# Recurrence step of a fused two-layer kernel: the power's exponent split in two, and the carrier's matmuls doubled into two PSUM banks

## The reference

```python
h_carrier = h.mean(axis=1)                      # over the 256 channels
T = cos((phase(xr_t) - phase(h_carrier)) / 2) ** 2
alpha = exp(dt_t * A_neg)
expo = 1 + (1 - alpha) * 0.5 * (1 - T)
mag, ph = c_mag(h), c_phase(h)                  # c_mag: sqrt(re^2 + im^2 + 1e-8)
cmag = minimum(exp(expo * log(mag + 1e-8)), 10)
h = from_polar(cmag, ph) + B_t * (dt_t * x_t)
h = from_polar(tanh(c_mag(h)), c_phase(h))
y_t = einsum('bnc,bdnc->bd', C_t, h)
```

## Time and profile before

| | |
|---|---|
| median of 3 runs | 12826.88 us (12825.58 to 12827.23) |
| the profiled execution | 12837.53 us |
| its span, first to last instruction | 12835.7 us |
| busy: DVE, ACT, PE, PEld | 76%, 64%, 45%, 33% |
| mean granted PE clock | 0.613 of full speed |

### The profile page before, as it was taken

One profiled execution on the slowest core, in us unless ns is written; L12 is line 12 of the kernel. 1 busy time (PEld: TensorE's weight loads), 2 busy tenths in 40 slices (PEclk: granted clock), 3 DMA queues, 4 the chain that ended last, 5 costly groups with the idle time before them and its releaser, 6 DMA issues. The chain is left out here.

```text
span 12835.7 us, 220415 instructions
## 1 busy us (share of the span) xinstructions
PE 5755.6 (45%) x52526; PEld 4270.2 (33%) x52542; DVE 9759.4 (76%) x56587; ACT 8162.1 (64%) x42451; POOL 94.5 (1%) x164
## 2 busy tenths in 40 slices
PE   5222222222222222222222222222237978888998
PEld 5222222222222222222222222222234546653335
DVE  5777777777777777777777777777774948868875
ACT  6666666666666666666666666666663732264665
POOL 0000000000000000000000000000000100000000
PEclk8555555555555555555555555555558979998999
DMA  1000100001000000001000010000100000011100
GB/s 56 14 14 14 21 14 14 14 14 21 14 14 14 18 17 15 14 14 20 16 14 14 14 21 14 14 14 14 21 10 12 1 23 6 1 37 48 31 24 21
DMA packets 339459, 227.53 MB, mean 18 GB/s; under 512 B 27662, under 2 KB 324183, under 8 KB 337884
## 3 DMA queue, kind: packets, MB, share of 16 engines
q1 hardware_dynamic: 338140, 213.30, 7.8%
HBM read 187.41 MB, written 25.43 MB: 17 GB/s over the span
## 5 line engine op out<-in xcount | busy, mean ns | idle before, releaser
L534 PE MATMUL scan_p_car<-scan_hs,scan_mean_mat 32*32 32x2 f32 x16392 | 579.6, 198 | 6583.9 <-DVE scan_hb L661 6571.2
L534 PEld LDWEIGHTS scan_p_car<-scan_hs,scan_mean_mat 32*32 32x32 f32 x16392 | 403.7, 136 | 6762.8 <-DVE scan_hb L661 6749.9
L579 ACT ACTIVATE scan_act_ps<-scan_act_ps 128x64 f32<-128x64 f32 (+1 forms) x8193 | 1635.1, 200 | 65.5
L579 ACT ACTIVATE scan_act_ps<-scan_state_ps 128x64 f32<-128x64 f32 x2048 | 426.0, 208 | 1879.4 <-DVE scan_state_ps L658 1879.4
L561 PE MATMUL scan_p_y<-scan_c_masked,scan_hb 128*64 128x4 f32 x16384 | 1234.2, 253 | 0.0
L539 PE MATMUL scan_p_car<-scan_eps_row,ones 1*128 1x3 f32 x4102 | 1197.9, 360 | 39.1 <-DMA scan_a_log<-L_attn_a_A_log 38.9
L661 DVE SCALAR_TENSOR_TENSOR scan_uw<-scan_w,scan_rsq 128x64 f32<-128x64 f32 x2048 | 461.4, 225 | 853.4 <-ACT scan_rsq L579 853.4
L561 PEld LDWEIGHTS scan_p_y<-scan_c_masked,scan_hb 128*64 128x64 f32 x16384 | 1055.4, 216 | 34.2
L539 PEld LDWEIGHTS scan_p_car<-scan_eps_row,ones 1*128 1x128 f32 x4102 | 1020.4, 308 | 72.0 <-DMA scan_a_log<-L_attn_a_A_log 39.3
L579 ACT ACTIVATE scan_power_ps<-scan_state_ps,scan_s 128x64 f32<-128x64 f32 x2049 | 591.1, 288 | 673.3 <-DVE scan_s L684 673.3
L658 DVE TENSOR_TENSOR scan_c<-scan_V,scan_power_ps 128x64 f32<-128x64 f32 x4096 | 723.7, 218 | 366.8 <-ACT scan_power_ps L579 304.7
(11 more groups left out here) (450 smaller groups left out, 17412.8 us busy)
## 6 DMA issues: line engine op xcount, KB each, us to landing
scan_step_in<-scan_scratch SPq DMA_DIRECT2D x520, 256.0 KB, 6.2
qk_scratch<-qkv_parts SPq DMA_DIRECT2D x32, 384.0 KB, 2.5
attn_qT<-qk_scratch SPq DMA_DIRECT2D x192, 64.0 KB, 2.2
attn_kT<-qk_scratch SPq DMA_DIRECT2D x192, 64.0 KB, 2.2
scan_scratch<-prep_dts SPq DMA_DIRECT2D x32, 256.0 KB, 2.1
x<-L_attn_a_x SPq DMA_DIRECT2D x1, 4096.0 KB
out<-x SPq DMA_DIRECT2D x1, 4096.0 KB
filter_in_taps<-c_kT SPq DMA_DIRECT2D x1, 2048.0 KB
```

The lines of the kernel that those rows point to most:

```text
L534: last = nc.tensor.matmul(p_car[slot][rows, 0:2], mean_mat[rows, :], hs[rows, :], start=False, stop=True)
L579: nc.scalar.activation(dst, src, func, **kw).then_inc(counts[par]["act"], 1)
```

## The change

The exponential's argument is split: `exp(-(alpha - 5) * lm / 4)` becomes an ACT instruction of its own (`pw`), and the rest, `exp((alpha - 1) * lm * dot * rs)` (the quarter is in the table behind `dot`), takes `rs` itself as pointer scale. `s` goes; DVE gets `t = (alpha - 5) * lm` and `X = dl * dot` (pointer scalar `dot`, written to PSUM). `F` and the wide `V` go; in their place are `Vr0`, `Vr1` (state times `ru`) and `V0`, `V1` (times `pw`), and `hp` is gone since `Vr0` adds the epsilon itself. `lm` moves ahead of `nsq` on ACT, and `mag` is written to PSUM. The carrier's four matmuls are made twice, into a bank for ACT and one for DVE, so `dot` waits for PE's `carrier2` in place of ACT's `nsq`. Both banks are seeded each step by two `epsilon` calls, behind `nsq` and `dot` and ahead of `y`.

```diff
-DVE_STEP = [..., "h0", "h1", "nh", "hp", "dot", "F", "dl", "s", "V"]
-ACT_STEP = [..., "l2", "mag", "lnh", "nsq", "ru", "lnn", "lm", "rs", "cm"]
-PE_STEP = ["carrier", "y"]
+DVE_STEP = [..., "h0", "h1", "nh", "dot", "dl", "t", "X", "Vr0", "Vr1", "V0", "V1"]
+ACT_STEP = [..., "l2", "mag", "lnh", "lm", "nsq", "ru", "lnn", "rs", "pw", "cm"]
+PE_STEP = ["carrier", "carrier2", "y"]
...
+        mag, pw = M, ln2
+        r2, X = (state_ps[:, q * J:(q + 1) * J] for q in range(2))
+        n2, nh, t = (norm_ps[:, q * J:(q + 1) * J] for q in range(3))
+        p_car = {who: ph.ps(f"p_car_{who}", [P, 512]) for who in ("act", "dve")}
...
+                def carrier(par):
+                    for who in ("act", "dve"):
+                        for q in range(4):
+                            rows = slice(32 * q, 32 * q + 32)
+                            last = nc.tensor.matmul(p_car[who][rows, 0:2], mean_mat[rows, :], hs[rows, :], start=False, stop=True)
+                        last.then_inc(counts[par]["pe"], 1)
+                def epsilon(start=True):
+                    for who in ("act", "dve"):
+                        nc.tensor.matmul(p_car[who][:, 0:3], env["ones"][0:1, :], eps_row[:, :], start=start, stop=not start)
...
                             after(pe, "dve", "h1", par, k)
-                            carrier(par, slot)
-                            epsilon(1 - slot)
+                            carrier(par)
+                            after(pe, "act", "nsq", par, k)
+                            after(pe, "dve", "dot", par, k)
+                            epsilon()
                             for half in range(2):
...
                     op(par, lnh[:, :], nh[:, :], ACT.Ln)
+                    after(act, "act", "mag", par, k)
+                    op(par, lm[:, :], mag[:, :], ACT.Ln, bias=EPS_MAG)
                     after(act, "pe", "carrier", par, k)
-                    op(par, squares[:, :], p_car[slot][:, 0:3], ACT.Square, accum_out=nsq[:, :])
+                    op(par, squares[:, :], p_car["act"][:, 0:3], ACT.Square, accum_out=nsq[:, :])
                     after(act, "act", "lnh", par, k)
                     op(par, ru[:, :], lnh[:, :], ACT.Exp, scale=-0.5)
                     after(act, "act", "nsq", par, k)
                     op(par, lnn[:, :], nsq[:, :], ACT.Ln)
-                    after(act, "act", "mag", par, k)
-                    op(par, lm[:, :], mag[:, :], ACT.Ln, bias=EPS_MAG)
                     after(act, "act", "lnn", par, k)
                     op(par, rs[:, :], lnn[:, :], ACT.Exp, scale=-0.5)
-                    after(act, "dve", "s", par, k)
-                    op(par, cm[:, :], dl[:, :], ACT.Exp, scale=s_[:, 0:1])
+                    after(act, "dve", "t", par, k)
+                    op(par, pw[:, :], t[:, :], ACT.Exp, scale=-0.25)
+                    after(act, "act", "rs", par, k)
+                    after(act, "dve", "X", par, k)
+                    op(par, cm[:, :], X[:, :], ACT.Exp, scale=rs[:, 0:1])
...
-                    nc.vector.tensor_scalar(hb[:, slot, 0, :], hb[:, slot, 2, :], EPS_PHASE, None, ALU.add).then_inc(sem, 1)
-                    after(dve, "act", "nsq", par, k)
-                    stt(sem, products[:, :], p_car[slot][:, 0:2], 1.0, tab[:, nxt, k_nxt, 2:4], ALU.mult, ALU.mult, accum_out=dot[:, :])
-                    after(dve, "act", "ru", par, k)
-                    stt(sem, F[:, :], mag[:, :], EPS_MAG, ru[:, :], ALU.add, ALU.mult)
+                    after(dve, "pe", "carrier2", par, k)
+                    stt(sem, products[:, :], p_car["dve"][:, 0:2], 1.0, tab[:, nxt, k_nxt, 2:4], ALU.mult, ALU.mult, accum_out=dot[:, :])
                     after(dve, "act", "lm", par, k)
                     stt(sem, dl[:, :], alpha[:, (k + 1) % 2, :], 1.0, lm[:, :], ALU.subtract, ALU.mult)
-                    after(dve, "act", "rs", par, k)
-                    after(dve, "dve", "dot", par, k)
-                    nc.vector.tensor_scalar(s_[:, :], rs[:, :], dot[:, 0:1], -0.25, ALU.mult, ALU.add).then_inc(sem, 1)
-                    after(dve, "dve", "F", par, k)
-                    tt(sem, V[:, :, :], hb[:, slot, 0:2, :], F[:, :].unsqueeze(1).to_broadcast([P, 2, J]), ALU.mult)
+                    stt(sem, t[:, :], alpha[:, (k + 1) % 2, :], 5.0, lm[:, :], ALU.subtract, ALU.mult)
+                    after(dve, "dve", "dl", par, k)
+                    nc.vector.tensor_scalar(X[:, :], dl[:, :], dot[:, 0:1], None, ALU.mult).then_inc(sem, 1)
+                    after(dve, "act", "ru", par, k)
+                    stt(sem, Vr[:, 0, :], hb[:, slot, 2, :], EPS_PHASE, ru[:, :], ALU.add, ALU.mult)
+                    tt(sem, Vr[:, 1, :], hb[:, slot, 1, :], ru[:, :], ALU.mult)
+                    after(dve, "act", "pw", par, k)
+                    for comp in range(2):
+                        after(dve, "dve", f"Vr{comp}", par, k)
+                        tt(sem, V[:, comp, :], Vr[:, comp, :], pw[:, :], ALU.mult)
...
                             after(dve, "act", "cm", par, k - 1)
-                            after(dve, "dve", "V", par, k - 1)
                             for comp in range(2):
+                                after(dve, "dve", f"V{comp}", par, k - 1)
                                 tt(sem, c[:, comp, :], V[:, comp, :], cm[:, :], ALU.mult)
```

More of the change, by code:

```diff
@@ L402, in _ @@
                     nc.vector.tensor_tensor(xr[1], xr[1], xrs[:, :], ALU.mult).then_inc(soft_done, 1)
-DVE_STEP = ["c0", "c1", "w0", "w1", "sq0", "sq1", "na", "r2", "n2", "bx0", "bx1", "uw0", "uw1", "h0", "h1", "nh", "hp", "dot", "F", "dl", "s", "V"]
-ACT_STEP = ["al", "l", "M", "ln2", "E", "rsq", "L1", "R", "th2", "l2", "mag", "lnh", "nsq", "ru", "lnn", "lm", "rs", "cm"]
-PE_STEP = ["carrier", "y"]
+DVE_STEP = ["c0", "c1", "w0", "w1", "sq0", "sq1", "na", "r2", "n2", "bx0", "bx1", "uw0", "uw1", "h0", "h1", "nh", "dot", "dl", "t", "X", "Vr0", "Vr1", "V0", "V1"]
+ACT_STEP = ["al", "l", "M", "ln2", "E", "rsq", "L1", "R", "th2", "l2", "mag", "lnh", "lm", "nsq", "ru", "lnn", "rs", "pw", "cm"]
+PE_STEP = ["carrier", "carrier2", "y"]
 STEPS = {"dve": (DVE_STEP, "h0"), "act": (ACT_STEP, "l2"), "pe": (PE_STEP, "carrier")}
@@ L448, in scan_phase @@
         hb = ph.sb("hb", [P, 2, 3, J])
-        c, w, sq, uw, bx, V = (ph.sb(n, [P, 2, J]) for n in ("c", "w", "sq", "uw", "bx", "V"))
-        na, rsq, R, th2, mag, ru, F = (ph.sb(n, [P, J]) for n in ("na", "rsq", "R", "th2", "mag", "ru", "F"))
+        c, w, sq, uw, bx, Vr, V = (ph.sb(n, [P, 2, J]) for n in ("c", "w", "sq", "uw", "bx", "Vr", "V"))
+        na, rsq, R, th2, ru, dl = (ph.sb(n, [P, J]) for n in ("na", "rsq", "R", "th2", "ru", "dl"))
         act_ps, state_ps, norm_ps, power_ps = (ph.ps(n, [P, 512]) for n in ("act_ps", "state_ps", "norm_ps", "power_ps"))
         lr, E2, ln2, M, L1, l2, lnh = (act_ps[:, q * J:(q + 1) * J] for q in range(7))
-        r2, dl = (state_ps[:, q * J:(q + 1) * J] for q in range(2))
-        n2, nh = (norm_ps[:, q * J:(q + 1) * J] for q in range(2))
+        mag, pw = M, ln2
+        r2, X = (state_ps[:, q * J:(q + 1) * J] for q in range(2))
+        n2, nh, t = (norm_ps[:, q * J:(q + 1) * J] for q in range(3))
         lm, cm = (power_ps[:, q * J:(q + 1) * J] for q in range(2))
@@ L457, in scan_phase @@
         squares, nsq, lnn = act_ps[:, 448:451], act_ps[:, 456:457], act_ps[:, 464:465]
-        dot, s_, rs = (ph.sb(n, [P, 1]) for n in ("dot", "s", "rs"))
-        p_car = [ph.ps(f"p_car{k}", [P, 512]) for k in range(2)]
+        dot, rs = (ph.sb(n, [P, 1]) for n in ("dot", "rs"))
+        p_car = {who: ph.ps(f"p_car_{who}", [P, 512]) for who in ("act", "dve")}
         p_y = [ph.ps(f"p_y{k}", [P, 512]) for k in range(2)]
@@ L528, in _ @@
                 pe.wait_ge(start, 3)
[L530 to L541, removed]
+                def carrier(par):
[8 more added lines that the diff above has]
+                epsilon()
                 before_step_0(pe, "pe")
                 after(pe, "dve", "h1", 1, CS - 1)
-                carrier(1, 1)
-                after(pe, "pe", "carrier", 1, CS - 1)
+                carrier(1)
+                after(pe, "pe", "carrier2", 1, CS - 1)
                 pe.sem_inc(counts[1]["pe"], 1)
-                epsilon(0)
+                after(pe, "act", "nsq", 1, CS - 1)
+                after(pe, "dve", "dot", 1, CS - 1)
+                epsilon()
                 with pe.Fori(0, NCH // CHUNKS) as i:
@@ L565, in _ @@
                             leave(pe, k)
-                epsilon(0, start=False)
+                epsilon(start=False)
             @block.scalar
```

## The result

The changed kernel takes 13037.8 us (median of 4 runs, 13028.57 to 13043.18) against 12826.23 us before (median of 4): 211.6 us slower, a ratio of 1.0165, 95% interval 1.0147 to 1.0183. I forecast slower, 12,940 in 12,860 to 13,070. The direction is as forecast; the size is nearly double: +212 where I had +114.

A forecast was written before the change was run, and what follows sets the result against it. DVE and ACT, taking turns, bound the kernel, so only the start of `c` mattered. 1984 steps x 0.03 (59 us), 64 chunk ends x 0.81 (52) and 5 us of stalls made 116, giving 12,940, range 12,860 to 13,070.

The forecast's parts named there:

- What bounds the step: Recurrence step of 4.49 us: only the start of `c` matters; what follows takes 2.43 us whatever happens before.
- ACT and the exponentials: On ACT, `lm` starts at 0.80, 0.3 earlier; `Square` moves to about 0.92, `rs` runs to about 1.50, late for nothing.
- The sign that I named: In the trace after, ACT's wait ahead of `cm` would be for `X`; no size given.
- PE and `dot`: Second matmul set adds 0.10 to 0.21; `products` starts between 0.85 and 1.05, taken as 0.94 against 1.04.
- rival 2: Second matmul set 0.21 late: `products` at 1.05, `c` at 2.20; 13,060 (to 13,160); chance 0.20.
- DVE's queue becomes the path: Seven DVE instructions from `products` to `c`, `X` to `Vr0` 0.20: `c` at 2.09, 0.03 later, 61 us slower.
- The step that was mis-sized: On DVE, `Vr0` to `Vr1` 0.14, then 0.135 each to `V0`, `V1` and `c`, which starts at 2.09 to 2.10.
- The end of each chunk: Last step of a chunk: `y` behind both seeds delays `output`, `c` 0.81 later; 64 chunks, 52 us (45 to 63).
- Stalls in issue: DVE has three more instructions a step; some 5 us go on stalls in issue.
- Steps even, chunk ends only: `X` at 0.16, `c` at 2.05 to 2.06, only the chunk ends cost: 12,880; chance 0.18.
- Faster: Release of `dl` sets `c`: `dl` at 1.05, `X` at 0.16, `c` at 2.03 or 1.97; 12,695 to 12,797; chance 0.08.
- Cancelled: `c` at 2.03 to 2.04 pays for the chunk ends: within 26 us of before; chance 0.08.

The follow-up runs named there:

- e7: Changed kernel with only the two waits ahead of `cm` exchanged (`X` first, `rs` second): 13037.35 us in one run.
- e5: Changed kernel with PE making DVE's set of carrier matmuls first and ACT's second: 13021.24 us in one run.
- e3: Changed kernel with `X` in SBUF instead of PSUM: 12975.72 us, ratio 1.0127 against the kernel before.
- e1: Changed kernel with the two waits at `V0` and `c0` swapped, DVE's own result first, ACT's second: 12884.94 us, ratio 1.0057 against the kernel before.
- b1: Kernel before the change with the two waits ahead of `c0` exchanged, `V` first and `cm` second: 12952.21 us, ratio 1.0107.
- e2: Changed kernel with PE's `y` matmuls ahead of the waits on `nsq` and `dot` and the two seeds: 12968.05 us, ratio 1.0123 against the kernel before.
- e6: Kernel of e4 with the two waits ahead of `cm` also exchanged (`X` first, `rs` second): 12788.84 us, ratio 0.997 against the kernel before.
- e4: Changed kernel with waits at `V0` and `c0` swapped, `y` ahead of the seeds and `X` in SBUF: 12831.43 us, ratio 1.001 against the kernel before.
- b3: Kernel before with two carrier banks, `lm` ahead of `Square`, `dl` ahead of `F`, `y` ahead of the seeds, exponent not split: 13007.93 us in one run.

## Why the prediction came out as it did

- **What bounds the step.** Right. `c`'s start moved, and what follows it took 2.43 us before and after.
- **ACT and the exponentials.** Right: `lm` 0.79 to 1.00, `Square` at 0.91, `rs` over at 1.52, `pw` over at 1.64 and so not late for `V0` (e7: nor is `cm`). The sign that I named, ACT waiting for `X` ahead of `cm`, is not in the list: `pw` keeps ACT busy until 0.03 before `cm`.
- **PE and `dot`.** I took 0.94 from 0.85 to 1.05; it was 0.89. Coming second cost 0.10 (e5), the lower end of my 0.10 to 0.21, so the mechanism of rival 2 did not occur. The Trainium skill, "TensorEngine Tiling (Array Packing)", Key Properties, pointed to the lower end, and the trace agrees; that the 0.21 ahead of the seeds is such a drain is shown by no run here. `dl` was 0.04 earlier than I had it, and there `lm` holds it (e5).
- **DVE's queue becomes the path.** Right (e3), with 0.19 from `X` to `Vr0` against my 0.20. What the Trainium skill, "VectorE: DVE Perf Modes", section Why PSUM operands drop a tier, says of PSUM agrees with e3: `X` takes 0.281 into PSUM and 0.248 into SBUF.
- **The step that was mis-sized** is "`Vr0` to `Vr1` 0.14, to `V0` 0.135, to `V1` 0.135, to `c` 0.135". It is 0.13, 0.19, 0.14, 0.19. I took the distance of instructions that wait for one thing. Ahead of `V0` and `c0` stands a lone wait, on a result of DVE that had ended only shortly before. That is 2 x 0.053 = 0.106 a step. Of it 0.07 came back elsewhere (0.04 at `dl`, 0.03 in the other distances), so `c` started at 2.13 and not at 2.09 to 2.10. The steps grew by 0.073 where I forecast 0.03: 1984 x 0.043 = 85 us more. e1 and b1 show the mechanism. A hint of it stood in the trace before:

```profile
5004.03 0.26 ACT L579 ACTIVATE scan_th<-scan_R 128x64 f32<-128x64 f32 x1
...
5004.39 0.23 DVE L661 SCALAR_TENSOR_TENSOR scan_norm_ps<-scan_hb,scan_th 128x64 f32<-128x64 f32 x1
```

`nh`, the second row, waits for `h0` and then `th2`, and starts 0.10 behind `th2`'s end, where single waits start 0.03 behind. It would not have settled it, since `nh` also stands only 0.06 behind the readout of `h1`'s sum, which might have set it as well.
- **The end of each chunk.** Mechanism right (e2), size too small: I had 0.81 for the last step, it was 0.95, 61 us for 52. `y` starts where I had it (2.12 for 2.09). The term that failed is the 0.66 from `y`'s start to `output`'s: it is 0.78, in the kernel before as well. I had read the old `output` as waiting for nothing. With 0.78 the same sum gives 2.87 for `output` and about 0.93 for the last step.
- **Stalls in issue.** 5 us forecast, not shown. 4 us of the accounts are unplaced, and the idle time that the list puts down to issue ahead of `c` from 1000 to 9000 us went from 38.1 to 40.1 us.
- **What was luck.** The time lies inside my range, but outside the 12,900 to 12,985 that my own mechanism gave. It lies where I had put rival 2, whose cause did not occur; the range holds it only because it took in part of that rival. The direction inside the steps was luck too. The queue as I walked it, with the distances that the trace has for instructions with one wait, puts `c` at 2.13 - 0.106 = 2.03, 0.03 earlier than before; this is an estimate, since one wait of each pair always stands alone. That would have gained about as much as the chunk ends lost, 65 us against 61. The whole slowdown inside the steps comes from the two lone waits, of which the forecast has nothing, and in e1, where one of them costs nothing and the other delays `c` by 0.03, the step is 4.489 against 4.493 before.
- **The rivals.** "Steps even, chunk ends only" fails on `X`, and would have failed without it: in e3 `X` goes at its 0.16 and the step is still 0.04 longer than before. "Faster" had the release of `dl` right, at 1.03, and failed on the distances behind it. Without the dear waits at `V0` and `cm`, the late `y` and the slow `X` it is what happens (e6), but only by 0.3%. "Cancelled" is e4 by number, not by its own mechanism.

Open: whether the exponents' split could give more with both conditions of `c0` in a single wait, and what `y` ahead of the seed would give in the kernel before by itself. Neither was tried. e5, e7 and b3 are single runs; what is read from them is the order of starts in their traces.

## What to carry to other kernels

Where an instruction waits for two things, the order of the calls decides which wait it carries itself and which is issued alone ahead of it, and here a lone wait that is met late cost about 0.07 us more than a carried one. Call first the wait for what comes last; and before adding steps to an in-order chain of 0.14 us instructions, count such pairs as instructions. A dependence moved off one engine's path gains only as far as the other's queue is empty behind it, so count what has to follow the new release. Work that is put ahead of a result whose only reader is far away in most steps can still be late for the one place, here the chunk's end, where the reader comes at once. And an instruction without idle time in the list can still have been released by another engine, as `output` was here: hold its distance from that engine's row against other places before calling it free.

## What the runs showed of the hardware

- A semaphore wait as an instruction of its own lasts 0.021 us on DVE and 0.017 on ACT in the records, but where it is met late the next instruction starts about 0.065 behind its start; from the awaited end to the reader it is 0.10, against 0.03 for a carried wait (b1: ratio 1.0107 from one pair exchanged).
- An fp32 pointer-scalar instruction on 64 columns takes 0.248 us into SBUF and 0.281 into PSUM on DVE; the same move makes ACT's reader dearer, 0.318 for a pointer-scale `Exp` from SBUF and 0.288 from PSUM.
- A second set of four small matmuls behind the first cost its reader 0.10 us (e5); PE's granted clock stayed at 0.50 while its busy share of the stretch rose from 29% to 41%.
- From the start of the eight `y` rows on PE to DVE's `output`, where `y` releases it, it is 0.78 us, in the kernel before and in the changed one alike.
